# Probabilities moved in four transfers of 128 rows instead of sixteen of 32, with keys or values reordered inside a tile

## What is computed

```
# layer 0: 8 key/value heads, rotary embedding, causal
x = x + layernorm(attention0(layernorm(x)))
x = x + layernorm(linear_with_lora(layernorm(x)))
# layer 1: 32 key/value heads, biases, rmsnorm on q and k, not causal
q, k, v = h @ Wq + bq, h @ Wk + bk, h @ Wv + bv      # per head: 512 x 128
q, k = rmsnorm(q, gq), rmsnorm(k, gk)
attn = softmax(q @ k.T * scale)                      # 512 x 512 for each head and batch
out = (attn @ v) @ Wo + bo
x = x + layernorm(out)
x = x + layernorm(swiglu_with_lora(layernorm(x)))
```

## Time and profile before

| | us |
|---|---|
| median of 3 runs | 2169.48 |
| range of the runs | 2168.19 to 2174.43 |
| the profiled execution | 2171.16 |
| its span, first to last instruction | 2169.2 |
| mean granted TensorE clock in it | 0.987 |
| layer 0, steady middle | about 88 for a pass of 32 steps |
| SyncE busy with one set of sixteen moves, undisturbed | 10.0 |

### The profile page before, as it was taken

The page is one execution under the profiler, slowest core; times in us unless marked ns, Lnnn a source line. Parts: engine busy times, 40 slices in busy tenths (PEclk is TensorE's granted clock), DMA queues, the critical chain, the costliest instruction groups (busy, mean ns, idle before and its releaser), DMA issues.

```text
span 2169.2 us, 37874 instructions
## 1 busy us (share of the span) xinstructions
PE 2081.9 (96%) x10535; PEld 1751.8 (81%) x10535; DVE 1629.3 (75%) x2969; ACT 1349.3 (62%) x3638; POOL 1230.4 (57%) x990
## 2 busy tenths in 40 slices
PE   6999999999999879999999999999999999979998
PEld 5788888888888657888888888888888888857787
DVE  6778888787888766877777778777777878876422
ACT  5877777777777546666565656666565656645321
POOL 3878787697786554554454645454454645356300
PEclk9999999999999989999999999999999999999999
DMA  2634444444444523555544455444544444562210
GB/s 84 136 101 121 115 104 124 104 119 114 118 105 123 133 68 79 113 116 113 114 116 102 104 118 115 103 107 109 127 111 99 107 113 103 130 150 87 88 54 25
DMA packets 219134, 231.69 MB, mean 107 GB/s; under 512 B 100528, under 2 KB 130384, under 8 KB 218992
## 3 DMA queue, kind: packets, MB, share of 16 engines
q1 hardware_dynamic: 218992, 229.97, 44.3%
HBM read 114.23 MB, written 6.55 MB: 56 GB/s over the span
## 4 chain that ended last, share of the span: by engine, by line
PE 71%; POOL 12%; issue 6%; DVE 4%; SPq 3%; ACT 2%; DMA 1%; POOLq 0%; DVEq 0%; ACTq 0%
PE l_general L83 13%; PE l_general L84 13%; PE l_general L85 13%; PE l_score L83 4%; PE l_out L83 4%; PE l_score L85 4%; PE l_score L84 4%; PE l_out L84 4%; PE l_out L85 4%; POOL l_rope L2257 3%; PE l_general L823 2%; POOL l_probsT_lo L90 2%; POOL l_qT_lo L90 2%; SPq L756 2%; PE ffn_h L83 2%
## 5 line engine op out<-in xcount | busy, mean ns | idle before, releaser
L90 POOL TENSOR_TENSOR l_probsT_lo<-l_moved,l_probsT_hi 128x512 fp32r<-128x512 f32 (+2 forms) x261 | 286.6, 1104 | 287.3 <-ACT l_probsT_hi L966 261.5
L960 ACT ACTIVATE l_probs<-l_score,l_negtop 128x512 f32<-128x512 f32 x256 | 176.1, 688 | 362.2 <-DVE l_negtop L1136 352.3
L90 DVE TENSOR_TENSOR l_probsT_lo<-l_moved,l_probsT_hi 128x512 fp32r<-128x512 f32 x251 | 281.0, 1120 | 30.8 <-ACT l_probsT_hi L966 30.4
L1136 DVE TENSOR_REDUCE l_negtop<-l_score 128x1 f32<-128x512 f32 x256 | 175.6, 686 | 91.3 <-PE l_score L85 88.9
L2059 ACT ACTIVATE l_probs<-l_score,l_negtop 128x128 f32<-128x128 f32 (+3 forms) x256 | 134.9, 527 | 168.3 <-DVE l_negtop L2172 167.5
L83 PE MATMUL l_out<-l_w_out_lo,l_oT_hi 128*128 128x512 f32 x512 | 208.2, 407 | 2.9 <-DVE l_oT_lo L90 2.9
L83 PE MATMUL l_score<-l_kT_lo,l_qT_hi 128*128 128x512 f32 (+3 forms) x512 | 190.3, 372 | 19.6 <-POOL l_qT_lo L90 8.3
L2172 DVE CUSTOM_DVE_ANT_0 l_score<-l_score,l_mask 128x128 f32<-128x128 f32 (+3 forms) x256 | 125.9, 492 | 109.5 <-PE l_score L85 108.2
L85 PE MATMUL l_out<-l_w_out_hi,l_oT_hi 128*128 128x512 f32 x512 | 201.1, 393 | 0.0
L84 PE MATMUL l_out<-l_w_out_hi,l_oT_lo 128*128 128x512 f32 x512 | 201.0, 393 | 0.0
L83 PE MATMUL l_general<-l_w_qk_lo,xT_hi 128*128 128x512 f32 x504 | 197.4, 392 | 0.0
(11 more groups left out here) (251 smaller groups left out, 6237.5 us busy)
## 6 DMA issues: line engine op xcount, KB each, us to landing
l_moved<-l_blocks SPq DMA_DIRECT2D x1024, 64.0 KB
l_moved<-l_blocks SPq DMA_DIRECT2D x512, 80.0 KB
l_inv_all<-inv_rows SPq DMA_DIRECT2D x32, 512.0 KB, 4.1
l_raw_out<-l_wo SPq DMA_DIRECT2D x64, 256.0 KB, 4.1
l_inv_all<-inv_rows SPq DMA_DIRECT2D x64, 256.0 KB, 3.6
l_raw_q<-l_wq SPq DMA_DIRECT2D x32, 256.0 KB, 4.1
l_raw_qk<-l_wq SPq DMA_DIRECT2D x64, 128.0 KB, 2.9
l_raw_qk<-l_wk SPq DMA_DIRECT2D x64, 128.0 KB, 3.0
```

Source lines behind the costliest of these rows:

```text
L90: return engine.tensor_tensor(out, full, hi.bitcast(F32), ALU.subtract)
L960: act.activation(probs[:, n % NPR], score[n % 2][:], ACT.Exp, bias=negtop[:, n:n + 1], accum_out=total[:, n:n + 1]).then_inc(s_exp, 1)
L1136: dve.tensor_reduce(negtop[:, n:n + 1], score[n % 2][:], AXX, ALU.max, negate=True)\
```

## The change

Each of the four partition groups g is now moved by one transfer: 32 source partitions with four blocks each, in order, fill 128 destination partitions, in order. So block c of partition 32g + y lands on partition 4y + c, where before it landed on 32c + y. The keys of a tile have to be in that order on one side: either the columns of the scores are permuted, or the rows of the values. In layer 1 the transpose of the keys writes token 4y + c to column 32c + y of its tile (`keys`), so that the probabilities land in the order of the tokens. Layer 0 masks by the place of a key, so its keys stay and the values are permuted: the copy to `v_turn` reads the bank in its order and writes with a step of four (`by_key`, `by_place`). The count of the semaphore for a set of moves falls from 256 to 64 (`MOVES`).

```diff
-MOVES = TB * TB * 16
+MOVES = TB * 16
@@ layer 1
+        def keys(rows):
+            return rows.rearrange("p (c y) -> p y c", c=TB)
...
                 for g in range(TB):
-                    for c in range(TB):
-                        sp.dma_start(moved[32 * c:32 * c + 32, k, g],
-                                     blocks[32 * g:32 * g + 32, k, c]).then_inc(s_move[k], 16)
+                    sp.dma_start(moved[:, k, g], blocks[32 * g:32 * g + 32, k]).then_inc(s_move[k], 16)
...
                     for t in range(TB):
-                        last = pe.transpose(bank[:, t * P:(t + 1) * P], y[:, b, t, at:at + HD], ident[:])
+                        to = bank[:, t * P:(t + 1) * P]
+                        last = pe.transpose(to if kind == "tq" else keys(to), y[:, b, t, at:at + HD], ident[:])
@@ layer 0
+        def by_place(rows):
+            return rows.rearrange("p (k y c) -> p k c y", k=TB, c=TB)
+
+        def by_key(bank):
+            return bank.rearrange("p (k c y) -> p k c y", k=TB, c=TB)
...
                 for g in range(TB):
-                    for c in range(TB):
-                        sp.dma_start(moved[32 * c:32 * c + 32, k, g],
-                                     blocks[32 * g:32 * g + 32, k, c]).then_inc(s_move[k], 16)
+                    sp.dma_start(moved[:, k, g], blocks[32 * g:32 * g + 32, k]).then_inc(s_move[k], 16)
...
-                act.activation(v_turn[:], bank_of(m, x, d)[:], ACT.Copy).then_inc(s_act, 1)
+                act.activation(by_place(v_turn[:]), by_key(bank_of(m, x, d)[:]), ACT.Copy).then_inc(s_act, 1)
```

## The result

The changed kernel took 2167.84 us, the median of 20 runs (2163.06 to 2170.33); the kernel before, beside it, 2174.14 us (2168.19 to 2178.80, 20 runs). The ratio is 0.9971, 95% interval 0.9963 to 0.9978, so the change is worth 6.3 us, between 4.8 and 8.0. The forecast was 4.8 us of gain and a time of 2165 us. The three runs that the forecast started from lay low: their median was 2169.48 us, 4.7 us under that of the twenty.

What follows compares the result with a forecast made beforehand. TensorE, busy 96% of the span, was taken to bound the kernel, with gains only at the layers' ends. 2.5 us (layer 1) plus 2.3 (layer 0) made 4.8 off the three-run median 2169.48: 2165 us, range 2157 to 2177.

Steps and rivals of the forecast that it cites:

- What bounds the kernel: Whole kernel: TensorE, busy 96% of the span; only the ends of the two attention layers can answer to faster moves.
- Issue: SyncE's queue, both layers: four moves of 0.59 us, so 2.4 us a set in place of 10.0.
- Transfer: Both layers: a set lands in 7 us (layer 1) or 9 us (layer 0), so 4 to 7 us sooner.
- My 6.9 us: Time from issue to landing of 1 MB transfers, taken as one alone; basis of the 7 us for layer 1.
- The bad end, 11.2: Layer 1: slowest landing allowed for a set, from a 1 MB transfer beside a set of moves.
- End of layer 1: VectorE's wait for slot 5's set 2.0 us, ScalarE's for slot 4's 0.8, less 0.3 for small waits: 2.5 us won.
- The clock: End of layer 1: products after the gap stay at the lower clock, costing 0 to 2.8 us; none counted back.
- End of layer 0: Sooner output weights 2.0 us, sooner moved set 0.3 us: 2.3 us won, between 0 and 6.
- VectorE's wait for the root: End of layer 0: 1.97 us for GpSimd's root of the first row norm; sooner output weights worth 2.0 us here.
- The order of keys and values: Layer 0's value copies and layer 1's key transposes, written with a step: zero cost; copies hidden even at twice the time.
- the rival of stepped writes: Layer 1's 256 key transposes write PSUM slower: up to 31 us, less 4.8 won, 2196 us; chance 0.18.
- The signs: Expected in the trace: 0.6 us issues, waits gone or under 1 us, slot 5's gap 5 to 6 us, middle unchanged.

Runs made afterwards that it cites:

- after_again: The changed kernel itself, unaltered, profiled a second time and timed again beside the kernel before: 2168.24 us, ratio 0.9980.
- copies_early: The changed kernel with the copies of slot 5's moved set earlier in the orders of ScalarE, GpSimd and VectorE: 2167.29 us, ratio 0.9965.
- set5_first: The changed kernel with slot 5's set sent ahead of the wait for slot 4's row sums and the load of x: 2167.60 us, ratio 0.9977.
- both together: The changed kernel with the edits of copies_early and set5_first: 2165.45 us, ratio 0.9961; a second time 2162.85 us, ratio 0.9963.
- rows_later: The changed kernel with the 1 MB load of x behind slot 5's set on SyncE's queue instead of ahead: 2167.97 us, ratio 0.9979.
- layer1_only: Layer 1 as in the changed kernel, layer 0 as in the kernel before: 2169.14 us, ratio 0.9985.
- order_alone: The kernel before with the new order of keys and values, still sixteen moves a set, to every fourth partition: 2173.94 us, ratio 0.9995.

## Why the prediction was right, point by point

**What bounds the kernel** held. The middle of layer 1 has the same length, and from 1000 to 1880 us no kernel's lag moved by more than 1.02 us, either way and in the kernel before too (0.87). All that repeats lies in the two ends.

**Issue.** 2.4 us a set was wrong: 4.2 us in layer 1 and 5.1 in layer 0 (medians in after_again). The price of a move of 32 rows was right for the first two of a set, 549 and 596 ns; what the sum lacked is that the third and fourth take 1.2 to 1.9 us. It was harmless. Eight moves with 5.49 us a set took the same time, since what holds SyncE now is the wait for row sums.

**Transfer.** 9 us in layer 0 came to 9.8 at the end (below) and 9.3 in the median of its sets. 7 us in layer 1 was wrong for the set that matters: 15.8 us in the first profile, 12.9 in the second, 14.6 in copies_early. It takes about what sixteen moves took (13.7 us) and is there sooner mainly because it leaves 6 to 8 us sooner. Sent ahead of the row sums' broadcast and the load of x, it took 7.7 to 7.9 us (set5_first and both together). So what the term lacked lies in what is queued just ahead of the set. It is not the load of x alone (12.3 us in rows_later); more these profiles do not separate. My 6.9 us was also misread as "one alone". It is the median of two loads of 1 MB issued half a microsecond apart at the start of the kernel, which took 5.7 and 8.2 us. The bad end, 11.2, was not bad enough.

**End of layer 1.** The two pieces were 2.0 and 0.8 us, less 0.3. The table's columns 1880-1910 and 1910-1922 give -0.9 and -1.45 in five of six profiles, with a gap of 6.07 us, just above the 5 to 6 forecast: what is late next is ScalarE's order, 0.55 us later than the VectorE time that I had taken. The gap of 4.08 us stayed (4.08 before 1941.52 in after_again). Against the mean of the profiles with sixteen moves the gain is 2.7 us; the sum had 2.5, and measured alone the layer gives 1.3 to 5.2. That 2.7 lies so near to 2.5 is partly luck. Against the profile that it was read from, the sum's terms gave 2.4 in five profiles and 0.2 in one. What the sum lacked is that the landing scatters: the profile before was one of its two best cases.

**The clock.** I counted no clock either way, and these two profiles show a place where it is lost. TensorE waits some 2.5 us near 1978 in both kernels; in before it comes back at full clock (granted clock 1.00 from 1980.7 to 1984), in after at half (0.50 from 1977 to 1980, 1.2 GHz), for seven products. Before, then after:

```profile
1980.71 0.47 PE L400 MATMUL ffn_merge<-ffn_side,ffn_tile 96*128 96x512 f32 x1 [2.53 <-DVE ffn_w_far_words L460]
1981.02 0.39 PE L83 MATMUL ffn_h<-xT_lo,ffn_w_near 128*128 128x512 f32 x1
```
```profile
1977.06 0.76 PE L400 MATMUL ffn_merge<-ffn_side,ffn_tile 96*128 96x512 f32 x1 [2.54 <-DVE ffn_w_far_words L460]
1977.62 0.63 PE L83 MATMUL ffn_h<-xT_lo,ffn_w_near 128*128 128x512 f32 x1
```

In the column 1922-1990 the six profiles with few moves and this order of copies lose 2.4 to 3.4 us, the four with sixteen moves -0.1 to 2.3. So in the profiles some 2.2 of the 2.7 us won at the end of layer 1 are handed back. The timed runs of layer1_only (1.3 to 5.2 us of gain) show less of that, and have no records of products to look at. Whether the giving back belongs to the change or to the profiled executions stays open.

**End of layer 0.** Second profile of the changed kernel, against the earlier trace rows:

```profile
713.35 1.93 SPq L1821 DMA_DIRECT2D l_raw_out<-l_wo  x1
...
722.23 4.97 SPq L1848 DMA_DIRECT2D l_moved<-l_blocks  x4
...
720.56 0.63 ACT L2005 ACTIVATE l_w_out_hi<-l_raw_out 128x512 fp32r<-128x512 f32 x1 [0.65 <-DMA l_raw_out<-l_wo]
...
724.07 0.50 PE L83 MATMUL l_score<-l_w_v_lo,l_w_k_hi 128*128 128x512 f32 x1 [0.76 <-DVE l_raw_q L1593]
...
732.70 0.21 DVE L154 TENSOR_SCALAR lin_norm_bias<-lin_norm_mean_var,lin_norm_rstd 128x1 f32<-128x1 f32 x1 [1.03 <-POOL lin_norm_rstd L148]
...
732.03 1.04 ACT L2072 ACTIVATE l_probsT_hi<-l_moved 128x512 fp32r<-128x512 f32 x2 [2.65 <-DMA l_moved<-l_blocks]
...
749.98 0.63 PE L1508 MATMUL l_score<-ident,l_trig 128*128 128x128 f32 x4 [2.89 <-DVE xT_lo L90]
```

The output weights leave at 713.35 (712 forecast), the wait for them is 0.65 us (gone), the set lands 9.8 us after its first issue, and VectorE's wait for the root falls by 0.94 us of the 1.97. The table shows -1.82 to -1.85 us over 726 to 735 in each of the nine kernels with fewer moves in layer 0, close to the 2.0, and nothing like it in the others (-0.65 to +0.19). A term that I lacked stands in front of it: +1.04 to +1.09 us over 700 to 726 in the same nine and in no other. There TensorE waits for a buffer `l_raw_q` that VectorE works on, 0.76 us. Before, then in after_again:

```profile
721.40 0.68 DVE L90 TENSOR_TENSOR l_probsT_lo<-l_moved,l_probsT_hi 128x512 fp32r<-128x512 f32 x1
722.61 0.64 DVE L90 TENSOR_TENSOR l_probsT_lo<-l_moved,l_probsT_hi 128x256 fp32r<-128x256 f32 x1
721.55 2.02 POOL L90 TENSOR_TENSOR l_probsT_lo<-l_moved,l_probsT_hi 128x384 fp32r<-128x384 f32 x2 [3.09 <-ACT l_probsT_hi L2066]
```
```profile
720.04 1.51 DVE L90 TENSOR_TENSOR l_probsT_lo<-l_moved,l_probsT_hi 128x512 fp32r<-128x512 f32 x1
722.07 1.34 DVE L90 TENSOR_TENSOR l_probsT_lo<-l_moved,l_probsT_hi 128x256 fp32r<-128x256 f32 x1
719.48 2.39 POOL L90 TENSOR_TENSOR l_probsT_lo<-l_moved,l_probsT_hi 128x384 fp32r<-128x384 f32 x2 [2.38 <-ACT l_probsT_hi L2072]
```

VectorE has no idle time ahead of its work on `l_raw_q`, so it does not wait for a late load. Two subtractions ahead of it take 1.5 and 1.3 us in each of the nine and 0.7 and 0.6 in each of the other five. In each of the nine GpSimd's first subtraction starts about 0.6 us ahead of VectorE's (719.48 and 720.04), in each of the five behind it (721.55 and 721.40). That GpSimd slows VectorE there is argued from these times; no run tests it. Over 735 to 760 the nine win 1.1 to 2.7 us, and the others lie between 0.6 lost and 1.8 won, all of it together with swings of the clock. In sum 700 to 760 gives 1.9 to 2.0 us in seven of the nine, 2.2 and 3.4 in the others; less the mean of the five with sixteen moves, which are 0.5 us ahead of the first profile, it is 1.6 us. The sum had 2.3 and the interval for this layer alone is 0.7 to 4.8.

**The order of keys and values.** Zero for the transposes was right, and the rival of stepped writes is refuted: 4230 products in 800 us, 108 ns from start to start in both kernels, order_alone at 0.9995. The Trainium skill, "SBUF — State Buffer", section "Door 1: The DMA port swizzle", says that any PSUM access that is not contiguous slows matmuls significantly; for these writes the trace disagrees. No run here shows a product other than a transpose that writes with a step. The same section gives SBUF lines of 16 bytes and says that each access that crosses to a new line pays a penalty. With a step of four words every word lies on a line of its own, and the copy, 591 to 1094 ns, agrees. "Even if each were twice as long it is hidden" was the case that came.

**The number.** Against the median of 2174.14 us the sum of 4.8 would have given 2169.3; measured were 2167.84. That is 1.5 us, and the measured gain of 4.8 to 8.0 us just reaches the sum; timed again (after_again) the gain was 4.3 us, 2.4 to 6.3, with the sum inside. So no term need be short, and none is shown to be. By the profiles the balance is another than mine: about 1.6 us at the end of layer 0, 1.0 between 760 and 1000 us and 2.7 at the end of layer 1, less 2.2 given back behind it. That the total agrees with a sum that had neither the give-back nor the clock is in part luck. 2165 itself lies 2.8 us from the measured time because the three runs it was taken from lay 4.7 us low and the gain was 1.5 us larger.

**The signs.** Four of those named came: the gap ahead of slot 5's product (6.07 us, just over the 5 to 6), the gap near 1941 (4.08), four transposes in 0.60 us, the middle at its length. Three did not: a median near 0.6 us and a set in 2.4 us; the waits for moved probabilities under 1 us (3.2 and 2.65 us at the end of layer 0, 2.35 in one profile of layer 1); no wait for output weights (0.4 to 0.65 us are left).

## What to carry to other kernels

Fewer, larger DMAs in one queue are worth what they let leave sooner, and only at the places where something waits for it; look for the queue's next in-order wait (here the row sums) before halving once more, because it takes over as soon as issuing is short. When a transfer comes sooner, the instruction that takes it stands in a fixed order made for the late one. Move both together: set and copies earlier gave the fastest kernel, 2 to 5 us more by the medians, either of them alone nothing that could be measured, and with sixteen moves less than nothing. And read a wait for a DMA from several executions: one profile before and one after would have put layer 1's gain at nothing, while the kernels changed in one layer give it about half.

## What the runs showed of the hardware

What a DMA's issue costs SyncE went by its place in a burst more than by its rows or bytes. A move of 32 rows and 64 KB took 513 to 592 ns at every place in a set of sixteen (medians). Of four moves that fill 128 partitions the first two took 549 and 597 ns, with 256 KB and with 320 KB, the third and fourth 1.2 and 1.7 us (256 KB) and 1.9 us (320 KB). With eight moves the medians were 603 ns (128 KB) and 768 ns (160 KB). Moving the same bytes by a quarter of the DMAs made the DMA engines busier, not less busy (0.50 to 0.65 in the middle of layer 1), and other loads later: the row sums' broadcast of 512 KB has a median of 6.5 us to landing with four moves, 5.4 with eight and 4.2 in order_alone. A set of four moves of 256 KB landed 7.7 to 7.9 us after its first issue where it was sent ahead of the row sums' broadcast, and after 12.3 to 15.8 us where it was sent behind it (slot 5, end of layer 1). A row of 2 KB behind a burst came back 9.7 us after its issue (1882.08 to 1891.74 in after_again). An activation that writes fp32 with a step of four words takes 1.85 times as long; a transpose of 128 columns that writes PSUM with a step of 32 words takes no longer (108 ns from start to start).
